# First and last tile of a two-layer residual kernel: finer load waits, second tile's hidden product ahead, weight splits spread over VectorE and GpSimd, last layer norm block by block

## What is computed

```python
x = x + layernorm(x + relu(x @ W1[l] + b1[l]) @ W2[l] + b2[l]) * gamma[l] + beta[l]   # l: language of the batch
ctx    = causal_ema(x, tau_ctx)                                # along the tokens
gated  = x * sigmoid(concat([x, ctx]) @ Wg.T + bg)
mod    = 0.5 + sigmoid(gelu(x @ Wn1.T + bn1) @ Wn2.T + bn2)    # 8 values a token
traces = [causal_ema(gated * mod[d], tau[d]) for d in range(8)]
temporal = sum_d traces[d] * softmax(blend)[d]
gate   = sigmoid(temporal @ Wtemp.T + btemp)
soma   = gelu(x @ Wsoma.T + bsoma)
x = x + layernorm((soma * gate) @ Wout.T) * gamma + beta
```

## Time and profile before

| | |
|---|---|
| median of 3 runs | 1406.18 us (1404.89 to 1406.24) |
| profiled execution: time, span | 1405.91 us, 1404.1 us |
| PE, DVE, ACT, POOL busy | 96%, 72%, 37%, 27% of the span |
| PE busy in the first, second and last of 40 slices | 3, 5 and 5 tenths, 9 tenths or more in the others |

### The profile page before, as it was taken

One profiled execution on the slowest core, in us unless ns is written; L12 is line 12 of the kernel. 1 busy time (PEld: TensorE's weight loads), 2 busy tenths in 40 slices (PEclk: granted clock), 3 DMA queues, 4 the chain that ended last, 5 costly groups with the idle time before them and its releaser, 6 DMA issues.

```text
span 1404.1 us, 19538 instructions
## 1 busy us (share of the span) xinstructions
PE 1344.5 (96%) x7836; PEld 971.7 (69%) x7836; DVE 1013.3 (72%) x1493; ACT 516.1 (37%) x812; POOL 378.4 (27%) x295
## 2 busy tenths in 40 slices
PE   3599999999999999999999999999999999999995
PEld 2366867677686767868677686767768676786754
DVE  6967777777777867777786777777777786777463
ACT  2325234252433425244242533415243342524332
POOL 4414223041330514123031422304133041411112
PEclk8799999999999999999999999999999999999998
DMA  7345361735528172471715626173552807344250
GB/s 258 119 127 182 91 180 46 217 106 135 165 65 234 41 188 114 113 198 66 215 47 150 188 84 187 45 210 113 135 166 67 239 33 184 117 113 128 75 136 30
DMA packets 91485, 186.22 MB, mean 133 GB/s; under 512 B 9859, under 2 KB 14595, under 8 KB 87299
## 3 DMA queue, kind: packets, MB, share of 16 engines
q1 hardware_dynamic: 91394, 184.98, 45.0%
HBM read 134.61 MB, written 50.33 MB: 132 GB/s over the span
## 4 chain that ended last, share of the span: by engine, by line
PE 56%; DMA 12%; DVE 10%; issue 9%; ACT 4%; SPq 2%; POOL 2%; POOLq 0%; DVEq 0%
PE ring L848 38%; DMA g_blocks<-g_f 7%; PE Tp L1000 5%; DMA grep<-g_blocks 5%; DVE U L754 4%; PE ring L841 3%; PE Tp L1009 3%; SPq L325 2%; PE ring L1021 2%; PE Tp L848 1%; ACT U L479 1%; DVE x L692 1%; DVE V L697 1%; DVE g_f L763 1%; PE ring L868 1%
## 5 line engine op out<-in xcount | busy, mean ns | idle before, releaser
L754 DVE TENSOR_TENSOR U<-grep,w_qs 128x1024 f32<-128x1024 f32 x256 | 300.9, 1220 | 69.5 <-issue 35.5
L379 POOL TENSOR_TENSOR x<-grep,b_row 128x512 f32<-128x512 f32 x64 | 80.6, 1291 | 581.1 <-DMA grep<-in_x 581.1
L1000 PE MATMUL Tp<-U,Arep 128*32 128x256 f32 x2048 | 144.7, 386 | 2.3 <-DVE U L754 2.1
L485 ACT ACTIVATE g_f<-g_f 128x512 f32<-128x512 f32 x64 | 40.5, 632 | 266.8 <-DVE g_f L759 266.7
L388 POOL TENSOR_TENSOR grep<-grep,beta_row 128x512 f32<-128x512 f32 x64 | 81.0, 1301 | 157.7 <-DMA grep<-x_tiles 157.7
L848 PE MATMUL ring<-x1T_hi,Wsoma_hi 128*128 128x512 f32 x256 | 114.6, 448 | 0.0
L1000 PEld LDWEIGHTS Tp<-U,Arep 128*32 128x32 f32 x2048 | 54.2, 109 | 86.6 <-issue 53.9
L759 DVE TENSOR_TENSOR g_f<-ring,bg_row 128x512 f32<-128x512 f32 x64 | 44.1, 689 | 94.6 <-PE ring L848 94.4
L848 PE MATMUL ring<-Wg_hi,seq_hi 128*128 128x512 f32 x256 | 100.7, 393 | 8.7 <-DVE Wg_r L553 8.7
L848 PE MATMUL ring<-seq_hi,Wtemp_hi 128*128 128x512 f32 x256 | 106.8, 417 | 1.6 <-DVE seq_lo L642 1.6
L848 PE MATMUL ring<-Wout_hi,g_r 128*128 128x512 f32 x256 | 100.4, 392 | 3.8 <-DVE soma_r L650 3.8
(11 more groups left out here) (151 smaller groups left out, 2757.4 us busy)
## 6 DMA issues: line engine op xcount, KB each, us to landing
grep<-g_blocks SPq DMA_DIRECT2D x256, 256.0 KB, 4.2
grep<-in_xc SPq DMA_DIRECT2D x16, 1024.0 KB, 8.2
grep<-in_x SPq DMA_DIRECT2D x16, 1024.0 KB, 8.9
x_tiles<-x SPq DMA_DIRECT2D x16, 1024.0 KB, 7.5
g_blocks<-g_f SPq DMA_DIRECT2D x64, 256.0 KB, 3.9
grep<-x_tiles SPq DMA_DIRECT2D x16, 1024.0 KB, 4.8
out<-U SPq DMA_DIRECT2D x64, 256.0 KB, 2.0
gamma_row<-in_g SPq DMA_DIRECT2D x9, 256.0 KB, 7.2
```

The source lines that it names most:

```text
L379: nc.gpsimd.tensor_tensor(new[:, b, :], x_t[:, b, :], b2_row[:, :], ALU.add).then_inc(xb2_ready, 1)
L485: nc.scalar.activation(g[:, b, :], g[:, b, :], ACT.Sigmoid).then_inc(sig_ready, 1)
L754: V_.tensor_tensor(U[:, (n + 2) % 4, :, :], grep[b % 2][:, :, at], w_qs[:, hh, at].unsqueeze(1).to_broadcast([P, NI, HC]), ALU.mult).then_ ...
L1000: last = nc.tensor.matmul(Tp[b % 2][i * L:(i + 1) * L, at], Arep[:, b * NI + i, hh, :], U[:, (n + 2) % 4, i, :], start=(hh == 0 and c == 0 ...
```

## The change

- One semaphore for six language loads becomes four (W1 with b1, W2, b2, gamma0 with beta0), each waited for where it is used; b1 is issued before W2, and in the first batch x is issued ahead of gamma0 and beta0.
- xT of tile 1 is issued ahead of Wg's first half, and Wg's second half right behind it, both before Wn2 and the rows.
- Tile 1's h and its split are made in slot -1 behind tile 0's y, in place of slot 0.
- Low parts: split 0 moves on DVE from slot 0 to slot -1; split 2 goes between the first and second `input_sum` of slot 0, and in that slot `context_low` stands behind the second; split 3 moves from DVE to POOL, between its L379 and L382 of slot 0; split 1 stays on POOL but waits for tile 0's x1.
- Epow, Rpow (`span_tables`) move from DVE's start to the end of its slot 0 first-layer work.
- n1 waits for the first scan in place of the fourth.
- Tile 15: the last transpose of the traces stands before the second half of soma chunk 3; the first two out blocks begin with the first three chunks and are ended when the fourth is split; in slot 16 the layer norm is done per block, from PSUM, with POOL's power per block, and scaling and addition of x1 in one DVE instruction.

```diff
@@ groups_of
-            if has_next:
+            if has_next and k != 0:
                 order += [("h", k + 1, 0)]
...
                 order += [("y", k + 1, b) for b in range(NB)]
+            if k == -1:
+                order += [("h", 1, 0)]
@@ sync: load_language, first_loads
+                sp.dma_start(W1[:, :, :], w1[...]).then_inc(ld_w1, 16)
+                sp.dma_start(b1_col, b1[...]).then_inc(ld_w1, 16)
+                sp.dma_start(W2_raw[:, :], w2[...]).then_inc(ld_w2, 16)
+                sp.dma_start(b2_row[:, :], b2[...].to_broadcast([P, C])).then_inc(ld_b2, 16)
+                if batch == 0:
+                    load_x(0)
+                for row, src in ((gamma0_row, g0), (beta0_row, be0)):
+                    sp.dma_start(row[:, :], src[...].to_broadcast([P, C])).then_inc(ld_norm, 16)
...
                 load_language(0)
-                load_x(0)
                 load_split(0, wn1)
                 load_split(1, wsoma)
+                sp.wait_ge(full["h"], upto(1, 0, 0))
+                load_xT(1)
                 load_split(2, wg[0:C])
+                load_split(3, wg[C:2 * C])
@@ gpsimd
                     for b in range(NB):
                         nc.gpsimd.tensor_tensor(new[:, b, :], x_t[:, b, :], b2_row[:, :], ALU.add).then_inc(xb2_ready, 1)
+                    if k & 1:
+                        pool.wait_ge(ld_norm, 32 * ((k + 1) // 2 + 1))
+                    elif k == 0:
+                        pool.wait_ge(split_hi, 4)
+                        split_low(3)
...
                         pool.wait_ge(split_hi, 2)
+                        pool.wait_ge(x1_ready, upto(4, 0, NB - 1))
                         split_low(1)
...
+                if has_prev and not has_cur:
+                    for b in range(NB):
+                        pool.wait_ge(last_var, b + 1)
+                        nc.gpsimd.tensor_tensor(rstd1[:, b:b + 1], rstd1[:, b:b + 1], minus_half[:, b:b + 1],
+                                                ALU.pow).then_inc(rstd1_ready, 1)
@@ scalar
+                def hidden_high(tile):
+                    act.wait_ge(full["h"], upto(1, tile, 0))
+                    ps = bank_of("h", tile, 0)
+                    nc.scalar.activation(ps[:, :], ps[:, :], ACT.Relu, bias=b1_col).then_inc(h_ready, 1)
+                    act.wait_ge(h_ready, upto(1, tile, 0))
+                    if tile == 1:
+                        act.wait_ge(full["y"], upto(4, 0, NB - 1))
+                    nc.scalar.activation(hid_hi[:, :], ps[:, :], ACT.Identity).then_inc(hidhi_ready, 1)
...
-                if k == 0:
-                    split(3)
...
+                    if has_next:
+                        soma_gelu(3)
+                        trace_high(3)
+                    else:
+                        trace_high(3)
+                        soma_gelu(3)
                 if k == -1:
                     split(0)
                     split(1)
                     split(2)
+                    hidden_high(1)
+                    split(3)
@@ vector
-                if k == 0:
+                if k == -1:
                     split(0)
-                    split(2)
...
+                def last_output_centred(b):
+                    ps = bank_of("out", k - 1, b)
+                    at = 13 * (k - 1) + 2 * b
+                    dve.wait_ge(full["out"], upto(4, k - 1, b))
+                    V_.bn_stats(stats1[:, b, :], ps[:, :]).then_inc(ln1_step, 1)
+                    dve.wait_ge(ln1_step, at + 1)
+                    V_.bn_aggr(mv1[:, b, :], stats1[:, b, :]).then_inc(ln1_step, 1)
+                    dve.wait_ge(ln1_step, at + 2)
+                    V_.tensor_scalar(rstd1[:, b:b + 1], mv1[:, b, 1:2], EPS, None, ALU.add).then_inc(last_var, 1)
+                    V_.scalar_tensor_tensor(res[:, b, :], ps[:, :], mv1[:, b, 0:1], gamma1_row[:, :],
+                                            ALU.subtract, ALU.mult).then_inc(last_centred, 1)
+
+                def last_output(b):
+                    dve.wait_ge(rstd1_ready, TILES - 1 + b + 1)
+                    dve.wait_ge(last_centred, b + 1)
+                    dve.wait_ge(x1b_ready, upto(4, k - 1, b))
+                    V_.scalar_tensor_tensor(res[:, b, :], res[:, b, :], rstd1[:, b:b + 1], x1_back[:, b, :],
+                                            ALU.mult, ALU.add).then_inc(res_ready, 1)
+
+                if has_prev and not has_cur:
+                    last_output_centred(0)
+                    last_output_centred(1)
+                    last_output(0)
+                    last_output_centred(2)
+                    last_output(1)
+                    last_output_centred(3)
+                    last_output(2)
+                    last_output(3)
...
                     for b in range(NB):
                         input_sum(b)
+                        if k == 0 and b == 0:
+                            split(2)
+                        if k == 0 and b == 1:
+                            context_low()
...
-                if k == 0:
-                    split(3)
+                if k == -1:
+                    hidden_low(1)
+                elif k == 0:
+                    span_tables()
@@ tensor
+                def hidden(tile):
+                    ps = free_bank(pe, "h", tile, 0)
+                    pe.wait_ge(ld_xT, 16 * upto(1, tile, 0))
+                    if tile % 2 == 0:
+                        pe.wait_ge(ld_w1, 32 * (tile // 2 + 1))
+                    product(ps[:, :], lambda n: W1[:, n, :], lambda n: xT[:, n, :], NC, "h")
...
+                if k == -1:
+                    hidden(1)
                 if has_cur:
-                    pe.wait_ge(ema_ready, upto(4, k, NC - 1))
+                    pe.wait_ge(ema_ready, upto(4, k, 0))
...
+                if has_prev and not has_cur:
+                    pe.wait_ge(somalo_ready, upto(4, k - 1, NC - 2))
+                    output_begun(0, NC - 1)
+                    output_begun(1, NC - 1)
+                    pe.wait_ge(somalo_ready, upto(4, k - 1, NC - 1))
+                    output_ended(0)
+                    output_ended(1)
+                    for b in range(2, NB):
+                        output_begun(b, NC).then_inc(full["out"], 1)
...
-                    soma_ended(3)
-                    trace_by_channels(3)
+                    if has_next:
+                        soma_ended(3)
+                        trace_by_channels(3)
+                    else:
+                        trace_by_channels(3)
+                        soma_ended(3)
```

More of the change, by code:

```diff
@@ L298, in second_loads @@
             def second_loads():
-                sp.wait_ge(full["h"], upto(1, 0, 0))
-                load_xT(1)
-                load_split(3, wg[C:2 * C])
                 sp.wait_ge(x1_ready, upto(4, 0, NB - 1))
@@ L448, in slot @@
                     if k & 1:
[L449 removed]
+                        act.wait_ge(ld_w2, 16 * ((k + 1) // 2 + 1))
                         nc.scalar.activation(W2[0][:, :], W2_raw[:, :], ACT.Identity).then_inc(w2hi_ready, 1)
[L451 to L455 removed]
+                    if k != 0:
+                        hidden_high(k + 1)
                 if has_prev:
@@ L467, in slot @@
                     nc.scalar.activation(hid[:, :], inner_bank[:, :], ACT.Gelu, bias=col[:, 0:1]).then_inc(h1_ready, 1)
-                if has_prev:
+                if has_prev and has_cur:
                     for b in range(NB):
@@ L651, in soma_gated, with hidden_low @@
                                      ALU.subtract).then_inc(somalo_ready, 1)
+                def hidden_low(tile):
+                    dve.wait_ge(hidhi_ready, upto(1, tile, 0))
+                    V_.tensor_tensor(hid_lo[:, :], bank_of("h", tile, 0)[:, :], hid_hi[:, :].bitcast(F),
+                                     ALU.subtract).then_inc(hidlo_ready, 1)
                 def context_low():
@@ L704, in input_centred @@
                 def input_centred(b):
+                    if b == 0 and k & 1:
+                        dve.wait_ge(ld_norm, 32 * ((k + 1) // 2 + 1))
                     V_.scalar_tensor_tensor(new[:, b, :], new[:, b, :], mv0[:, b, 0:1], gamma0_row[:, :],
@@ L724, in slot @@
                         input_centred(b)
-                if has_prev:
+                if has_prev and has_cur:
                     output_statistics(1)
-                if has_cur:
+                if has_cur and k != 0:
                     context_low()
-                if has_prev:
+                if has_prev and has_cur:
                     output_statistics(2)
@@ L902, in slot @@
                     temporal_gate(1)
-                if has_next:
-                    ps = free_bank(pe, "h", k + 1, 0)
-                    pe.wait_ge(ld_xT, 16 * upto(1, k + 1, 0))
-                    if odd:
-                        pe.wait_ge(ld_lang, 96 * ((k + 1) // 2 + 1))
-                    product(ps[:, :], lambda n: W1[:, n, :], lambda n: xT[:, n, :], NC, "h")
+                if has_next and k != 0:
```

(18 more changed lines are left out.)

38 lines of the change are left out of this document (16 added, 22 removed).

## The result

The changed kernel takes 1392.8 us (median of 4 runs, 1388.95 to 1395.9) against 1406.21 (1404.89 to 1409.79) of the kernel before on the same chip: ratio 0.9899, interval 0.9881 to 0.9917. That is 13.4 us less, where 21.6 were forecast, and 2.8 us above the upper end of the forecast range. The profiled execution took 1391.26 us, its span is 1389.3.

What follows compares the result with a forecast made beforehand. PE was taken to set the pace from 125 to 1360 us, so head and tail shifts add: 10.3 + 11.3 = 21.6 off 1405.91 gives 1384.3, with the median 0.27 higher 1384.6; range 1379.0 to 1390.0.

Steps and rivals of the forecast that it cites:

- step 3: Head, tile 0's x: overtakes two rows, 1.4 us; POOL starts at 17.0 in place of 18.35, additions end at 28.5.
- step 1: Head, h of tile 0: no wait for the last language row, start 14.05, 1.6 us gained.
- Step 4: Head, x1 of tile 0: ready at 34.1 in place of 40.8, a shift of 6.7 us.
- Step 7: Head, DVE from last scan to first gate: 16.6 us work plus 6.3 waits behind POOL; logits at 65.7, shift 10.4.
- Step 8: Head, PE meanwhile: waits for context_low until 54, but DVE is late by 6 us or more, covering PE's holes.
- Step 9: Head, gate to products: still 13.6 us, so first product shifts 10.4 and PE about 10.3.
- Tail: Last tile: 1.05 from the earlier transpose, 4.4 from out begun early, 5.8 from layer norm by block; 11.3 us saved.
- The head arrives at the end unchanged: Middle, 125 to 1360 us: PE sets the pace, so whatever the head saves or loses reaches the end unchanged.
- Rival 1: DVE mostly wins against POOL: first gate at 59.5 to 60.5, 5.4 us more saved, 1379.2; chance 0.17.
- Rival 2: New PE holes lower the clock, and more waits on DVE: head 6 to 8, total 1388; chance 0.22.
- Rival 3: x1 isn't earlier, from a late load or tile 1's xT holding PE: head 6, total 1388.9; chance 0.06.
- Rival 4: Slower: clock stays at half through tile 0's gates and sums, some 45 us of matmuls doubled, 1430; chance 0.03.

Runs made afterwards that it cites:

- the addition held: Changed kernel plus one wait: POOL's first addition of b2 to tile 0's x waits until DVE's small table operations end; 1387.44 us, ratio 0.9861.
- the run without it: Changed kernel without POOL's split 3, ScalarE writing zeros as the low part of Wg's second half; 1391.05 us, ratio 0.9892.
- tail alone: Kernel before with only the change's last-tile edits; 1396.73 us, ratio 0.9915.
- the thirteenth: Kernel where SP waits in each steady tile for the last reload of g before the store of x1 and next loads; 1404.53 us, ratio 0.9984.
- the waits put back: Changed kernel with later batches' language loads again on one semaphore and n1 waiting for four scans except in tile 0; 1394.03 us, ratio 0.9902.
- after again: The changed kernel word for word, run and profiled a second time; 1394.21 us, ratio 0.9905.

## Why the prediction missed, step by step

**Head, step 3: the step that failed.** It let x overtake two rows and counted the earlier start as a gain bounded by 0 from below. It gave x at 17.0 and, in step 2, the end of the tables at 17.4, and the text's own mechanism, that a DVE operation with two SBUF inputs waits for POOL's running one, stood a paragraph above; nobody asked what an addition at 17.0 does to DVE operations until 17.4. In truth x was ready for POOL 0.7 to 1.9 us sooner still (additions from 15.14 to 16.30 where the tables began by 9.3), and the chain's last operations are short and stand one behind the other, so that most pay a whole addition: 2 to 8 us where the gain was to be 1.4. In the three profiles of the changed kernel it is 5.1 us on average. One wait that takes it out gave 1387.44 against 1392.8 (or, by ratios to before, 0.9861 against 0.9899 and 0.9905): 5 to 6 us of the 8.2 us miss, with intervals of 2.5 to 4 us to each side of the three ratios. What is left is within the noise: 0.9861 [0.9839, 0.9883] of 1406.21 is 1386.7, from 1383.6 to 1389.8, and the forecast is 1384.6. It is within the middle's scatter too, below.

**Head, step 1** was right: h began at 12.97, sooner than the 14.05 said, with no wait for rows, and took 4.82 in place of 3.67, so that it ended at 17.79 where the forecast makes 17.7; nothing came of the rest, since DVE's low part was the later one. **Step 4** met its number by luck: x1 was ready at 34.2, forecast 34.1, but in the execution whose chain was 2 us too long. In the two others it was ready at 39.1 and 43.0, and with the addition held, where no operation of the chain is long, at 32.8 and 32.0. So step 4 was some 1.3 to 2 us too slow, and the delay of step 3 covered it in the first profile; POOL's eight additions ended at 27.6 with the hold, where 28.5 was said. **Step 5, tile 1's h:** no wait of PE for it; right. **Step 6:** the last scan ended at 43.08, forecast 42.8.

**Step 7: right mechanism, one wait mis-sized.** From the last scan to the first gate DVE took 24.4 us where 16.6 + 6.3 = 22.9 were said. Split 2 took 3.30, 1.0 of it wait (said 1.2). `context_low` waited 7.0, not 4.1: the rest of split 3 (3.3 by the run without it) and turns with the four additions of beta0 (3.7), which the forecast had as 1.0 on the centring; that took 2.74, with no wait. Net 1.5 too little, within the bounds given there (0 and 9). With the addition held, steps 4 and 7 nearly cancel, and that is why the 109.30 of its first profile lies so near 108.9. The prediction's page of the Trainium skill (SBUF — State Buffer, the part on the two physically separate sides) calls the SBUF port pair that VectorE and GpSimd share a lock held by whoever starts first; the trace agrees (9.48, 1.24), and shows besides that two engines with work in line take turns by instruction. Why some operations with SBUF inputs kept their time between two additions (L631 and L635, 0.15 to 0.18) isn't shown.

**Step 8** was right in its effect: PE waited 6.4 us for `context_low` and ran at a granted clock of 0.50 until 59.7 (matmuls 0.43 apart), all ahead of the first gate, which was bound by DVE. A second hole, 2.1 us before 69.73, was followed by the same spacing until 73.3; this too was off the path, as the next step's number shows. **Step 9** was exact: 81.07 - 67.50 = 13.57, said 13.6.

**Tail: right, term by term.** From the start of the last L1009/L1102 to temp 5.03 before (1360.57 to 1365.60) and 4.03 after: 1.0, said 1.05. From temp to out 13.99 and 11.29: 2.7, said 2.7. Out from first to last matmul 12.41 and 10.79: 1.6, said 1.7. After the last matmul 11.7 and 5.8: 5.9, said 5.8. Sum 11.2, said 11.3. The whole rest became only 10.3 shorter in the first profile, because the last L1009/L1102 came 75.4 us after tile 15's transposes in place of 74.4; in the other executions with the new tail the rest is 106.6 to 107.7, which is 10.2 to 11.3 less than 117.9. The tail alone measured 12.0 with an interval of 2.8 to each side. Inside, POOL's power on 128x1 took 0.55, not 1.45, and two scalings stood one behind the other (1.41), and the two errors cancel.

**"The head arrives at the end unchanged": true as a mechanism, too sure as a number.** The middle ran from 1166.4 to 1172.4 in twelve executions (the thirteenth, with its made wait, left out), of kernels with old and new steady tiles alike: 1167.0, 1170.1 and 1171.4 with the old ones, mean 1169.5; eight with the new ones, mean 1169.1; and 1169.5 with the waits put back. The tiles don't share it evenly. From tile 8's transposes to tile 9's it took 83.7 to 87.4 us and from tile 13's to tile 14's 82.9 to 86.0; together these two range over 5.8 us (166.6 to 172.4), the other twelve together over 3.1 (998.9 to 1002.0). In the longest, 87.4 in the tail alone, DVE waited 3.9 us for the last reload of g (1.6 in the 83.7 of the kernel with the held addition), PE then 1.8 us for the products, and from 782 to 786 us its granted clock was 0.57; in the 83.7 no wait of PE shows, and its clock was 1.00. The row of 2.1 us came from the quieter end of that. Why the reload lands late, and why there, was not found. By this alone a forecast made from one execution is open by some 3 us each way.

**The rivals.** Rival 1 fell (`context_low` 9.48). Rival 2 named more waits on DVE, up to 2.7, and 1388; the waits came (1.5 more than counted), but not through holes or the clock: the matmuls at 80 us are 0.23 apart. Rival 3 names one of the two totals nearest to the measured one (1388.9, still 3.9 below), by a cause that is the opposite of what happened: x came too early, not too late. Rival 4 fell. What was missing is a rival in which an earlier load starts an engine that blocks another one. The step that failed, in short: step 3 priced the earlier x at no cost, and the runs show a cost of 2 to 8 us in DVE's chain.

## To carry to other kernels

A transfer that lands earlier starts work earlier, and on GpSimd that work can cost VectorE more than it gains: before x is moved ahead, look at what VectorE does in that very stretch, and hold the GpSimd work behind a chain of short operations; one wait was worth about 5 us here. As a worst case, price a GpSimd instruction by its whole length for each VectorE operation on SBUF that meets it, and let back-to-back work on both take turns. Where the head ends in an engine's chain, compare several executions before a microsecond is put down to an edit.

## What the runs showed of the hardware

- Operations of 0.15 to 0.29 us on VectorE, down to 128x1, took 1.2 us each beside GpSimd's 128x512 additions (after again, 15.26 to 21.45), while some between them (L631, L635) kept 0.15 to 0.18. A semaphore wait between two of them isn't what makes the difference: L630 follows L629 without one and took 1.22. PSUM readers kept theirs (scan 1.21).
- Four `context_low` of 0.62 took 9.48 us beside a 128x2048 subtraction and additions on GpSimd, 6.22 beside additions alone; GpSimd pays as well: 6.64 for a split of 4.54, 8.38 for four additions of 5.0.
- GpSimd's power on 128x1 took 0.55 us where 128x4 takes 1.45.
- The first copy of the tables began between 7.7 and 11.6 us, whatever the kernel, so that even the start of a program moves by 4 us.
